# Cross-attention, last batch: softmax denominators of three slots from sums on GpSimd in place of products with ones

## The chip, the cores and the metric

One core of a Trainium2 chip runs the whole kernel. The metric is the device time of one execution in microseconds (us), the median of several runs. The core has TensorE (PE in the profile; PEld are its weight loads), VectorE (DVE), ScalarE (ACT), GpSimd (POOL) and SyncE (SP), which here only starts transfers. Each engine works its own instructions in order and waits for the others by semaphores.

## What is computed

A decoder layer for 8 batches of 224 rows of 512 values, with a context of 750 rows a batch: linear self-attention, cross-attention with 16 heads of 32, and a feed-forward network (FFN) with ternary weights. The change is inside cross-attention:

```python
q = heads(x_q @ w_q)
k, v = heads(x_kv @ w_kv)
logits = q @ k.T * SCALE + (i - j) * w_rel[head]
attn = softmax(logits)            # exp(logits - max) / sum over the 750 keys
x = x + (attn @ v) @ w_proj
```

The "denominator" of a query and head is that sum over keys.

## The kernel before

`cross_attention` works through B = 8 batches b, each in NG = 4 slots s of HG = 4 heads; the text counts slots as n = 4b + s, so the last batch is slots 28 to 31. A slot has 16 beats k. In each beat every engine has a fixed list of work, written out by hand, so that the beats order the engines against each other.

On TensorE a beat holds: one or two halves of the maxima of the *next* slot (`maxima_half`, read by VectorE in `reduce_half`, L1761); in beats 0 to 11 one `logits` (L1952), for key tile pair i = k // 4 and head j = k % 4, into one of two PSUM banks; in beats 5, 9 and 13 an `attend` (L1992) for i = 0, 1, 2; in beat 2 the `denominators` of the slot before (L2002); in beat 12 `turn_maxima`, which waits for VectorE's `join_maxima`; and one part of a projection from a table. In the last batch that table (`last_fill`) holds, besides keys (K) and outputs (Y), the parts W0 to W23: transposes of the FFN's ternary weights. W0 to W3 stand in beats 12 to 15 of slot 28, W4 to W7 in beats 6, 8, 10, 12 of slot 29, W8 to W15 in slot 30, W16 to W23 in beats 0 to 8 of slot 31.

ScalarE turns logits into exponentials (L1652), 125 keys x 448 (two key tiles a = 0, 1 of 224 queries), into one of two buffers of `pT`, i by i in turn. It also copies projections, and in the last batch scales and rounds the FFN weights (`round_weight`, L1643) five beats ahead of their W part, and issues the last six key copies itself at beat 13 of slot 29 (L1683). VectorE makes each rounded weight ternary two beats ahead of its W part (`ternary`, L1783, a TENSOR_SCALAR from SBUF to SBUF), and takes the transposed weight out of PSUM after it (L1725). At beat 2 it divides the slot before: `divide`, a reciprocal (L1774) and a product (L1777). GpSimd splits that result in two parts (`split_heads`, L1526 and L1528).

A denominator is made in one of two ways. In slots 0 to 27 GpSimd adds the six tiles of exponentials of a slot in five additions of 125 x 896 (`sum_keys`, L1543; the text calls them m0 to m4). m0 needs the exponentials of i = 0, m1 and m2 those of i = 1, m3 and m4 those of i = 2. TensorE then multiplies the one sum with ones in `denominators`, four products a slot. ScalarE's exponentials wait for `p_summed`, since the buffers of `pT` come free only when added. In slots 28 to 31 `attend` multiplies every tile with ones too, 24 products a slot, and `divide` waits for `pv_done`:

```python
for col in (0, DEN) if b == B - 1 else (0,):
    for j in range(HG):
        h = HG * s + j
        weights = cv[...] if col == 0 else ones[0:KB, 0:HD]
        last = M.matmul(psO[...], weights, pT[...], ...)
```

In the earlier batches VectorE's `normalise` (L1707), two TENSOR_SCALAR from SBUF to SBUF, comes at beat 12 of slot 3 of a batch, beside `sum_keys`.

The FFN starts behind slot 31. Its first rows are loaded by `first_x` into the space of the sums (`sum_space`), once `den_full` says that the last sum was read; VectorE's `ffn_statistics(0)` reads them at beat 7 of slot 31, and GpSimd's `ffn_prepare(0)` goes on from there.

Of the kernel before, what the change touches and what calls it, by code (L numbers as in the profile page):

```python
# [20 lines left out]
NG = D // P  # L21
# [27 lines left out]
def wait_apart(eng, sem, value, passed):  # L49

    eng.wait_ge(sem, value)
    eng.sem_inc(passed, 1)
# [1138 lines left out]
def cross_attention(nc, sems, sa, x1, ctx_rows, k_rows, q_rows, x2, shared, ffn_weights, w_abs, w_deq, out):  # L1191
# [5 lines left out]
    B, N, _ = x1.shape  # L1197
# [12 lines left out]
    DEN = 256  # L1210
# [2 lines left out]
    LAST_STEP = UNITS - HG  # L1213
    HALVES = 2 * NT * HG
    BEATS = 16
    EXP_BANKS = 2
    PROJ_BANKS = 3


    counts = (2, 1, 1, 1, 1, 1, 1, 2, 2, 1, 2, 1)  # L1220
    halves_at = [range(sum(counts[:k]), sum(counts[:k + 1])) for k in range(BEATS)]
    unit_at = [(k // HG, k % HG) if k < UNITS else None for k in range(BEATS)]
    attend_at = {5: 0, 9: 1, 13: 2}
    DENOMINATORS_AT = 2
# [27 lines left out]
    ]  # L1252
    unit_beat = {int(what[1:]): BEATS * s + k for s in range(NG) for k, what in last_fill[s].items() if what[0] == "W"}
    ROUND_AHEAD, TERNARY_AHEAD = 5, 2
# [24 lines left out]
    def ended_before(b, s, k):  # L1279

        s, k = (s, k - 1) if k > 0 else (s - 1, BEATS - 1)
        b, s = (b, s) if s >= 0 else (b - 1, NG - 1)
        part = part_at(b, s, k) if b >= 0 else None
        return part[:2] if part and part[2] == parts_of[part[0][0]] - 1 else None
# [13 lines left out]
    with ExitStack() as ctx:  # L1298
# [52 lines left out]
        ffn_eps = sb("ffn_eps", [P, 1])  # L1351
        psS = ps("psS", [P, EXP_BANKS, 512])
        psO = ps("psO", [P, 512])
# [14 lines left out]
        p_summed, den_full = sem("p_summed"), sem("den_full")  # L1368
# [8 lines left out]
        def ffn_part(unit):  # L1377

            n, t = weight_of(unit)
            w = ffn_weights[n].rearrange("(a p) k -> p a k", p=P)  # L1380
            src = w[:, 2 * t:2 * t + 2] if n < 2 else w[:, :, 2 * t * P:2 * (t + 1) * P]
            return f_raw[raw_of[unit]].rearrange("p (a k) -> p a k", a=src.shape[1]), src
# [7 lines left out]
        spare, = (n for n in range(PROJ_BANKS) if n not in [bank_of[what, B - 1] for what in ("Y0", "Y1")])  # L1390
        ffn_places = {"ident": ident_b, "magic": magic, "eps_half": ffn_eps, "sums": sum_space, "keys": k_st_space,
                      "packed_k": k4_space, "packed_q": q4_space, "context": c_space, "banks": (psS, psM, psO, psR),
                      "sums_read": den_full, "sums_read_all": NG * (B - 1),
                      "output_banks": [bank_of[what, B - 1] for what in ("Y0", "Y1")],
                      "spare_read": (read[spare], len(order[spare::PROJ_BANKS])),
                      "outputs_read": [(read[bank_of[what, B - 1]], use_of[what, B - 1]) for what in ("Y0", "Y1")],
# [8 lines left out]
        def _(sp):  # L1405
# [38 lines left out]
            def load_ffn(unit):  # L1444

                if unit < 3:
                    sp.wait_ge(pv_done, NB * NG * (B - 1))
                elif unit == 3:
                    for pair in range(2):
                        wait_apart(sp, q_packed[pair], QPACK * B, sp_passed)  # L1450
                elif unit == 4:
                    for what in ("Xa", "Xb"):
                        wait_apart(sp, full[bank_of[what, B - 1]], use_of[what, B - 1], sp_passed)
                elif raw_before[unit] is None:
                    sp.wait_ge(full[bank_of["K3b", B - 1]], use_of["K3b", B - 1])
                else:
                    sp.wait_ge(f_tern_ready, raw_before[unit] + 1)
                dst, src = ffn_part(unit)
                sp.dma_start(dst, src).then_inc(f_in[raw_of[unit]], DMA)
# [36 lines left out]
                    pack_keys(b + 1, 1)  # L1496
                    pack_queries(b + 1, 1)
            ffn_first_x, ffn_rest = ffn_sync(sp)
            ffn_first_x()
            for unit in range(18, UNITS_W):  # L1500
                load_ffn(unit)
            ffn_rest()

        @block.gpsimd
        def _(pool):
# [65 lines left out]
            for b in range(B):  # L1571
                for s in range(NG):
                    if (b, s) != (0, 0):
                        split_heads(*((b, s - 1) if s > 0 else (b - 1, NG - 1)))
                    if s == 1 and b >= 1:
                        store(b - 1)
                    if s == 3 and b + 2 < B:
                        rstd(b + 2)
                    if b + 1 < B:
                        sum_keys(b, s)  # L1580
                    if b + 1 < B:
                        clear_shift(b, s)
                    if s == NG - 1 and b + 2 < B:
                        load_context(b + 2)
# [8 lines left out]
        def _(act):  # L1593
# [51 lines left out]
            def exponentials(b, s, i, j):  # L1645
                n = NG * b + s
                if j == 0 and NB * n + i >= 2:
                    act.wait_ge(pv_done, NB * n + i - 1)
                    if n < NG * (B - 1) or (n == NG * (B - 1) and i < 2):
                        act.wait_ge(p_summed, SUMS * n + (-2, 0, 1)[i])  # L1650
                act.wait_ge(st_full, UNITS * n + HG * i + j + 1)
                nc.scalar.activation(pT[:, (s + i) % 2, j], psS[0:KB, (HG * i + j) % EXP_BANKS, 0:2 * N],  # L1652
                                     ACT.Exp).then_inc(exp_done, 1)
# [9 lines left out]
            for b in range(B):  # L1663
                for s in range(NG):
                    for k in range(BEATS):
                        if ended := ended_before(b, s, k):
# [18 lines left out]
                        if b == B - 1:  # L1685
                            for unit in range(UNITS_W):
                                if unit_beat[unit] - ROUND_AHEAD == BEATS * s + k:
                                    round_weight(unit)
# [3 lines left out]
        def _(dve):  # L1692
# [74 lines left out]
            def divide(b, s):  # L1767

                n = NG * b + s
                if b < B - 1:  # L1770
                    dve.wait_ge(den_full, n + 1)
                else:
                    dve.wait_ge(pv_done, NB * (n + 1))
                V.reciprocal(den[:], psO[:, DEN:DEN + N]).then_inc(den_ready, 1)  # L1774
                dve.wait_ge(den_ready, n + 1)
                wait_count(dve, oT_ready, n)
                V.tensor_tensor(o_f[:], psO[:, 0:N], den[:], ALU.mult).then_inc(o_ready, 1)  # L1777
# [42 lines left out]
            for b in range(B):  # L1820
                for s in range(NG):
                    n = NG * b + s + 1
# [32 lines left out]
        def _(pe):  # L1855
# [86 lines left out]
            def logits(b, s, i, j):  # L1942
# [3 lines left out]
                if i == 0 and j == 0:  # L1946
                    pe.wait_ge(shift_ready, n + 1)
                wait_count(pe, exp_done, unit + 1 - EXP_BANKS)
                for a in range(2):
                    t = 2 * i + a  # L1950
                    col = t * KB if t < NB else t * KB + OVER
                    last = M.matmul(psS[0:KB, (HG * i + j) % EXP_BANKS, a * N:(a + 1) * N], k4[0:ROWS, s % 2, j, col:col + KB],  # L1952
                                    q4[0:ROWS, s, j, :], start=True, stop=True)
# [24 lines left out]
            def attend(b, s, i):  # L1978

                n = NG * b + s  # L1980
                pe.wait_ge(exp_done, UNITS * n + HG * (i + 1))
                if i == 0:
                    pe.wait_ge(w_scale_step, 1) if n == 0 else pe.wait_ge(o_ready, n)
                    for t in range(NK) if s == 0 else ():
                        pe.wait_ge(read[bank_of[f"V{t}", b]], use_of[f"V{t}", b])
                for a in range(2):
                    t = 2 * i + a
                    for col in (0, DEN) if b == B - 1 else (0,):
                        for j in range(HG):
                            h = HG * s + j  # L1990
                            weights = cv[:, b % 2, t, h * HD:(h + 1) * HD] if col == 0 else ones[0:KB, 0:HD]
                            last = M.matmul(psO[HD * j:HD * (j + 1), col:col + N], weights,  # L1992
                                            pT[:, (s + i) % 2, j, a * N:(a + 1) * N], start=t == 0 and col == 0,
                                            stop=t == NK - 1, skip_group_check=True)
                last.then_inc(pv_done, 1)
# [41 lines left out]
            for b in range(B):  # L2037
                for s in range(NG):
                    n = NG * b + s + 1
                    for k in range(BEATS):  # L2040
                        if n < NG * B:
                            for half in halves_at[k]:
                                maxima_half(n, half)
                            if k == TURN_AT:
                                turn_maxima(n)
                        if unit := unit_at[k]:
                            logits(b, s, *unit)
                        if k in attend_at:
                            attend(b, s, attend_at[k])
                        if k == DENOMINATORS_AT and 0 < NG * b + s <= NG * (B - 1):  # L2050
                            denominators(*((b, s - 1) if s > 0 else (b - 1, NG - 1)))
                        if part := part_at(b, s, k):
                            do(*part)
# [61 lines left out]
```

## Time and profile before

| | us |
|---|---|
| median of 3 runs (lowest, highest) | 1256.83 (1255.55, 1259.95) |
| the profiled execution, its own time | 1259.24 |
| its span, first to last instruction | 1257.4 |
| TensorE busy | 1174.2 |
| VectorE busy | 809.4 |
| ScalarE busy | 588.0 |
| GpSimd busy | 541.6 |

The span is what the profile covers; the time of the profiled execution has 1.84 us around it. Busy times overlap. Slot 28 begins at about 979 us of the span, slot 29 at 1002, slot 30 at 1024, slot 31 at 1046, and the FFN at about 1066. Timelines merge neighbouring instructions of one line, and a row's length is then that of the group.

### The profile page before, as it was taken

To read this page: it belongs to the slowest core of one execution; us is meant where nothing else is said; L and a number is where in the kernel's file an instruction comes from. 1 tells how busy PE (TensorE), PEld (TensorE's weight loads), DVE (VectorE), ACT (ScalarE), POOL (GpSimd) and SP (SyncE) were. 2 spreads that over 40 slices of the span, in tenths; PEclk is the share of its full clock that TensorE was granted. 3 is DMA by queue.
4 is the path that set the end of the run, shared out by engine and by line. 5 is a ranking of instruction groups with operands and counts; after the bars stand their busy time and mean duration, and the time that the engine had idled before them with its cause. 6 is when DMAs were issued, how large, how long until landed. Compare 5 with 4: busy or idle time off the path is not lost. (4 is left out here: it accounts for less than half of the span.)

```text
span 1257.4 us, 25102 instructions
## 1 busy us (share of the span) xinstructions
PE 1174.2 (93%) x9456; PEld 903.6 (72%) x9482; DVE 809.4 (64%) x1492; ACT 588.0 (47%) x967; POOL 541.6 (43%) x432
## 2 busy tenths in 40 slices
PE   3799999999799999999999999999999988899997
PEld 3687888887677878778877878878788866344443
DVE  5856666676546666656566665656665677587774
ACT  3222332225235445435444454444454566577775
POOL 0012111115116665656665665765755212354551
PEclk9899999999989999999999999999999989899999
DMA  5311333425524253343343343352532683122121
GB/s 173 96 49 47 102 127 127 143 79 165 134 74 114 51 149 96 73 125 89 80 133 98 82 133 86 97 138 52 134 101 60 202 247 113 42 73 67 58 67 42
DMA packets 76138, 129.43 MB, mean 103 GB/s; under 512 B 18764, under 2 KB 35276, under 8 KB 76027
## 3 DMA queue, kind: packets, MB, share of 16 engines
q1 hardware_dynamic: 63267, 104.28, 30.0%
q0 software_dynamic: 11680, 21.81, 5.4%
q10 hardware_dynamic: 1104, 2.15, 0.6%
q8 instruction: 58, 0.95, 0.3%
q14 instruction: 29, 0.24, 0.1%
HBM read 68.96 MB, written 11.22 MB: 64 GB/s over the span
## 5 line engine op out<-in xcount | busy, mean ns | idle before, releaser
L1761 DVE TENSOR_REDUCE xa_m_part<-xa_psM 112x1 f32<-112x376 f32 x512 | 266.5, 545 | 232.8 <-PE xa_psM L1968 230.3
L1652 ACT ACTIVATE space<-xa_psS 125x448 f32<-125x448 f32 x384 | 208.2, 544 | 180.7 <-PE xa_psS L1952 178.9
L1543 POOL TENSOR_TENSOR xa_sum_space<-xa_sum_space,space 125x896 f32<-125x896 f32 x112 | 238.3, 2128 | 97.3 <-ACT space L1652 92.9
L1968 PE MATMUL xa_psM<-xa_k,xa_q 104*112 104x376 f32 x512 | 162.2, 355 | 16.1 <-DVE xa_m_part L1761 7.6
L1952 PE MATMUL xa_psS<-xa_q,xa_k 104*125 104x224 f32 x768 | 147.3, 274 | 3.4 <-ACT space L1652 3.4
L1952 PEld LDWEIGHTS xa_psS<-xa_q,xa_k 104*125 104x125 f32 x768 | 139.1, 189 | 6.7 <-ACT space L1652 4.5
L1968 PEld LDWEIGHTS xa_psM<-xa_k,xa_q 104*112 104x112 f32 x512 | 87.9, 177 | 36.8 <-DVE xa_m_part L1761 12.9
L1526 POOL TENSOR_SCALAR xa_oT_hi<-xa_o_f 128x224 fp32r<-128x224 f32 x32 | 25.3, 790 | 180.7 <-DVE xa_o_f L1777 180.5
L1992 PE MATMUL xa_psO<-space,cv 125*32 125x224 f32 x1536 | 95.2, 360 | 0.9 <-ACT space L1652 0.9
L1938 PE MATMUL xa_psR<-xa_cT_hi,w_lo 128*128 128x376 f32 x256 | 91.6, 358 | 0.0
L1938 PE MATMUL xa_psR<-xa_cT_hi,w_hi 128*128 128x376 f32 x256 | 86.9, 339 | 1.7 <-DVE xa_cT_lo L1751 1.7
L1938 PE MATMUL xa_psR<-xa_cT_lo,w_hi 128*128 128x376 f32 x256 | 87.4, 341 | 0.0
L61 PE MATMUL sa_psR<-sa_xT_hi,w_hi 128*128 128x224 f32 x256 | 72.7, 284 | 10.8 <-DVE sa_xT_lo L472 10.8
L1938 PE MATMUL xa_psR<-w_hi,xa_cT_hi 128*125 128x512 f32 x192 | 79.9, 416 | 0.0
L1938 PE MATMUL xa_psR<-w_lo,xa_cT_hi 128*125 128x512 f32 x192 | 78.8, 410 | 0.0
L1938 PE MATMUL xa_psR<-w_hi,xa_cT_lo 128*125 128x512 f32 x192 | 76.6, 399 | 0.0
L1543 POOL TENSOR_TENSOR xa_sum_space<-space 125x896 f32<-125x896 f32 x28 | 59.7, 2132 | 28.6 <-ACT space L1652 24.2
L61 PE MATMUL sa_psR<-sa_xT_lo,w_hi 128*128 128x224 f32 x256 | 71.3, 279 | 0.0
L61 PE MATMUL sa_psR<-sa_xT_hi,w_lo 128*128 128x224 f32 x256 | 71.1, 278 | 0.0
L1595 ACT ACTIVATE cv<-xa_psR 125x512 f32<-125x512 f32 x48 | 28.7, 598 | 88.5 <-PE xa_psR L1938 88.5
L1992 PEld LDWEIGHTS xa_psO<-space,cv 125*32 125x32 f32 x1536 | 40.2, 109 | 30.7 <-issue 11.0
L1938 PEld LDWEIGHTS xa_psR<-xa_cT_hi,w_lo 128*128 128x128 f32 x256 | 49.1, 192 | 18.3 <-issue 18.3
(214 smaller groups left out, 2662.0 us busy)
## 6 DMA issues: line engine op xcount, KB each, us to landing
xa_k<-xa_k_st SPq DMA_DIRECT2D x378, 94.0 KB, 2.2
xa_q<-xa_q_st SPq DMA_DIRECT2D x192, 56.0 KB, 2.0
cv<-in_ctx_dram POOLq DMA_DIRECT2D x7, 1500.0 KB, 21.5
cv<-in_L_ffn_w_gate_dram SPq DMA_DIRECT2D x14, 512.0 KB, 4.7
cv<-in_L_ffn_w_down_dram SPq DMA_DIRECT2D x10, 512.0 KB, 7.0
cv<-in_L_ffn_w_up_dram SPq DMA_DIRECT2D x9, 512.0 KB, 6.0
sa_x_raw<-in_x_dram SPq DMA_DIRECT2D x8, 448.0 KB, 6.1
sa_rows<-in_x_dram SPq DMA_DIRECT2D x8, 448.0 KB, 4.0
```

The lines of the kernel that those rows point to most:

```text
L61: ins = nc.tensor.matmul(out, left(i, c), right(j, c), start=first and n == 0, stop=last and n == len(terms) - 1)
L1526: nc.gpsimd.tensor_scalar(oT_hi[:, s], o_f[:], 1.0, None, ALU.mult).then_inc(oT_hi_ready, 1)
L1543: nc.gpsimd.tensor_tensor(p_sum[:], before, tile, ALU.add).then_inc(p_summed, 1)
L1595: return nc.scalar.activation(out, in_, ACT.Copy, scale=scale)
L1652: nc.scalar.activation(pT[:, (s + i) % 2, j], psS[0:KB, (HG * i + j) % EXP_BANKS, 0:2 * N], ACT.Exp).then_inc(exp_done, 1)
L1761: V.tensor_reduce(m_part[:, t, jj, seg:seg + 1], psM[0:T, seg, 0:SEG], AX.X, ALU.max).then_inc(mx_read, 1)
L1938: last = M.matmul(out, left(i, k), right(j, k), start=m == 0, stop=m == len(terms) - 1)
L1952: last = M.matmul(psS[0:KB, (HG * i + j) % EXP_BANKS, a * N:(a + 1) * N], k4[0:ROWS, s % 2, j, col:col + KB], q4[0:ROWS, s, j, :], start=T ...
L1968: M.matmul(psM[0:T, seg, 0:SEG], q4[0:ROWS, g, jj, t * T:(t + 1) * T], k4[0:ROWS, g % 2, jj, seg * SEG:(seg + 1) * SEG], start=True, stop= ...
L1992: last = M.matmul(psO[HD * j:HD * (j + 1), col:col + N], weights, pT[:, (s + i) % 2, j, a * N:(a + 1) * N], start=t == 0 and col == 0, sto ...
```

## The change

Slots 28, 29 and 30 get their denominators as all slots before do: five additions on GpSimd, and four products of their sum with ones at beat 2 of the next slot. `attend` makes products with ones in slot 31 alone. ScalarE's exponentials of these slots wait for `p_summed`, `divide` of slots 28 to 30 waits for `den_full`, and the first load of FFN rows waits for `den_full` 31 in place of 28; on SyncE it is moved behind the loads of the weight parts 18 to 23.

```diff
--- before.py
+++ after.py
@@ -1213,6 +1213,7 @@
     LAST_STEP = UNITS - HG
     HALVES = 2 * NT * HG
     BEATS = 16
+    LAST = NG * B - 1
     EXP_BANKS = 2
     PROJ_BANKS = 3
 
@@ -1390,7 +1391,7 @@
         spare, = (n for n in range(PROJ_BANKS) if n not in [bank_of[what, B - 1] for what in ("Y0", "Y1")])
         ffn_places = {"ident": ident_b, "magic": magic, "eps_half": ffn_eps, "sums": sum_space, "keys": k_st_space,
                       "packed_k": k4_space, "packed_q": q4_space, "context": c_space, "banks": (psS, psM, psO, psR),
-                      "sums_read": den_full, "sums_read_all": NG * (B - 1),
+                      "sums_read": den_full, "sums_read_all": LAST,
                       "output_banks": [bank_of[what, B - 1] for what in ("Y0", "Y1")],
                       "spare_read": (read[spare], len(order[spare::PROJ_BANKS])),
                       "outputs_read": [(read[bank_of[what, B - 1]], use_of[what, B - 1]) for what in ("Y0", "Y1")],
@@ -1496,9 +1497,9 @@
                     pack_keys(b + 1, 1)
                     pack_queries(b + 1, 1)
             ffn_first_x, ffn_rest = ffn_sync(sp)
-            ffn_first_x()
             for unit in range(18, UNITS_W):
                 load_ffn(unit)
+            ffn_first_x()
             ffn_rest()
 
         @block.gpsimd
@@ -1576,7 +1577,7 @@
                         store(b - 1)
                     if s == 3 and b + 2 < B:
                         rstd(b + 2)
-                    if b + 1 < B:
+                    if NG * b + s < LAST:
                         sum_keys(b, s)
                     if b + 1 < B:
                         clear_shift(b, s)
@@ -1646,7 +1647,7 @@
                 n = NG * b + s
                 if j == 0 and NB * n + i >= 2:
                     act.wait_ge(pv_done, NB * n + i - 1)
-                    if n < NG * (B - 1) or (n == NG * (B - 1) and i < 2):
+                    if n < LAST or i < 2:
                         act.wait_ge(p_summed, SUMS * n + (-2, 0, 1)[i])
                 act.wait_ge(st_full, UNITS * n + HG * i + j + 1)
                 nc.scalar.activation(pT[:, (s + i) % 2, j], psS[0:KB, (HG * i + j) % EXP_BANKS, 0:2 * N],
@@ -1767,7 +1768,7 @@
             def divide(b, s):
 
                 n = NG * b + s
-                if b < B - 1:
+                if n < LAST:
                     dve.wait_ge(den_full, n + 1)
                 else:
                     dve.wait_ge(pv_done, NB * (n + 1))
@@ -1985,7 +1986,7 @@
                         pe.wait_ge(read[bank_of[f"V{t}", b]], use_of[f"V{t}", b])
                 for a in range(2):
                     t = 2 * i + a
-                    for col in (0, DEN) if b == B - 1 else (0,):
+                    for col in (0, DEN) if n == LAST else (0,):
                         for j in range(HG):
                             h = HG * s + j
                             weights = cv[:, b % 2, t, h * HD:(h + 1) * HD] if col == 0 else ones[0:KB, 0:HD]
@@ -2047,7 +2048,7 @@
                             logits(b, s, *unit)
                         if k in attend_at:
                             attend(b, s, attend_at[k])
-                        if k == DENOMINATORS_AT and 0 < NG * b + s <= NG * (B - 1):
+                        if k == DENOMINATORS_AT and NG * b + s > 0:
                             denominators(*((b, s - 1) if s > 0 else (b - 1, NG - 1)))
                         if part := part_at(b, s, k):
                             do(*part)
```

## Rows read from the trace of the kernel before

**Rows 1.** The page, costliest groups: xcount | busy us, mean ns | idle before, releaser.
```profile
L1761 DVE TENSOR_REDUCE xa_m_part<-xa_psM 112x1 f32<-112x376 f32 x512 | 266.5, 545 | 232.8 <-PE xa_psM L1968 230.3
```

**Rows 2.** Windows of slots 28, 29, 30: length, PE, PEld, DVE, ACT, POOL busy us, clock.
```profile
979.10:1002.30 23.20, 23.20 (x228) 18.80 (x226) 15.97 (x30) 12.99 (x20) 2.49 (x4) 1.00 0.63 192
...
1002.30:1023.70 21.40, 18.24 (x199) 14.62 (x195) 16.62 (x32) 12.26 (x19) 2.95 (x3) 1.00 0.76 225
...
1023.70:1046.20 22.50, 19.41 (x204) 14.99 (x204) 19.33 (x36) 18.42 (x24) 1.67 (x2) 0.85 1.07 316
```

**Rows 3.** Timeline of TensorE: start, us, line, what, [idle before <- releaser].
```profile
981.94 0.58 PE L2002 MATMUL xa_psO<-xa_sum_space,ones 125*32 125x224 f32 x8
...
986.30 0.56 PE L1992 MATMUL xa_psO<-space,ones 125*32 125x224 f32 x8
...
986.68 0.56 PE L1992 MATMUL xa_psO<-space,cv 125*32 125x224 f32 x8
...
1002.28 0.57 PE L1968 MATMUL xa_psM<-xa_k,xa_q 104*112 104x376 f32 x2
...
1023.66 0.60 PE L1968 MATMUL xa_psM<-xa_k,xa_q 104*112 104x376 f32 x2 [1.12 <-DMA xa_k<-xa_k_st]
...
1027.27 0.76 PE L1952 MATMUL xa_psS<-xa_q,xa_k 104*125 104x224 f32 x2 [1.56 <-ACT space L1652]
```

**Rows 4.** Timeline of ScalarE, last batch.
```profile
993.56 0.54 ACT L1652 ACTIVATE space<-xa_psS 125x448 f32<-125x448 f32 x1
...
998.11 0.53 ACT L1652 ACTIVATE space<-xa_psS 125x448 f32<-125x448 f32 x1
...
1013.24 0.54 ACT L1652 ACTIVATE space<-xa_psS 125x448 f32<-125x448 f32 x1 [1.09 <-PE xa_psS L1952]
...
1020.56 3.81 ACTq L1683 DMA_DIRECT2D xa_k<-xa_k_st  x6
...
1042.08 0.54 ACT L1652 ACTIVATE space<-xa_psS 125x448 f32<-125x448 f32 x1 [0.35 <-PE xa_psS L1952]
```

**Rows 5.** Timeline of VectorE, last batch.
```profile
997.08 0.69 DVE L1783 TENSOR_SCALAR xa_x_space<-cv 128x1024 bf16<-128x1024 f32 x1
...
1000.14 0.68 DVE L1725 TENSOR_SCALAR w_all<-xa_psR 128x1024 bf16<-128x1024 bf16 x1
...
1000.74 0.68 DVE L1783 TENSOR_SCALAR xa_x_space<-xa_q_st_space 128x1024 bf16<-128x1024 f32 x1
...
1008.78 0.68 DVE L1783 TENSOR_SCALAR xa_x_space<-xa_xn 128x1024 bf16<-128x1024 f32 x1
...
1012.31 0.69 DVE L1783 TENSOR_SCALAR xa_x_space<-cv 128x1024 bf16<-128x1024 f32 x1
...
1015.33 0.68 DVE L1783 TENSOR_SCALAR xa_x_space<-cv 128x1024 bf16<-128x1024 f32 x1
...
1034.89 0.55 DVE L1761 TENSOR_REDUCE xa_m_part<-xa_psM 112x1 f32<-112x376 f32 x1 [1.33 <-PE xa_psM L1968]
...
1043.59 0.68 DVE L1783 TENSOR_SCALAR xa_x_space<-cv 128x1024 bf16<-128x1024 f32 x1
...
1056.69 0.69 DVE L1725 TENSOR_SCALAR w_all<-xa_psR 128x1024 bf16<-128x1024 bf16 x1 [0.62 <-PE xa_psR L1895]
```

**Rows 6.** Timeline of GpSimd: additions of slot 3 and of slot 27.
```profile
444.12 4.51 POOL L1543 TENSOR_TENSOR xa_sum_space<-xa_sum_space,space 125x896 f32<-125x896 f32 x2 [2.38 <-ACT space L1652]
...
975.01 4.31 POOL L1543 TENSOR_TENSOR xa_sum_space<-xa_sum_space,space 125x896 f32<-125x896 f32 x2 [2.38 <-ACT space L1652]
```

**Rows 7.** Line 1707: duration in ns, shortest, median, longest.
```profile
L1707 DVE TENSOR_SCALAR xa_xn<-xa_xn,xa_x_mv,xa_x_rs x16: 531/545/2344, 313.4 to 886.8; 112x512 f32<-112x512 f32 x16
```

**Rows 8.** Timeline of VectorE in slot 3.
```profile
443.85 2.80 DVE L1707 TENSOR_SCALAR xa_xn<-xa_xn,xa_x_mv,xa_x_rs 112x512 f32<-112x512 f32 x2
```

**Rows 9.** Timeline of GpSimd in slot 29.
```profile
1008.55 1.44 POOL L1528 TENSOR_TENSOR xa_oT_lo<-xa_o_f,xa_oT_hi 128x224 fp32r<-128x224 f32 x1
```

**Rows 10.** Window of TensorE: length, busy us, granted clock, DMA share, GB/s.
```profile
1028.00:1030.00 2.00, 2.00 (x14) 0.50 1.04 280
```

## Prediction

> **What bounds the kernel now.** I read the page first. TensorE is its busiest engine, and the costliest group of instructions is VectorE's reduce of the maxima, L1761, which TensorE feeds and waits for by turns [rows 1]. But the change touches only the last batch of cross-attention, slots 28 to 31 (slot n = 4b + s), so what bounds those counts. The windows by slot give it [rows 2]: slot 28 has TensorE busy for 23.20 of 23.20 us and GpSimd for 2.49; slot 29 has TensorE at 18.24 of 21.40, VectorE at 16.62; slot 30 has TensorE at 19.41 of 22.50, VectorE at 19.33, ScalarE at 18.42. So slot 28 is bound by TensorE, and slot 30 by three engines in lock-step. GpSimd is nearly idle in all three. The timelines of single engines then show who hands to whom: in slots 29 and 30 TensorE stands still before the first logits of slot 30 for a packed key and then for ScalarE, which comes from issuing the key copies [rows 3, 4]; and VectorE works without a break from the end of slot 30 on, with the idle time 0.62 us near its last transposed weight of slot 31 [rows 5].
>
> **What is removed and added on TensorE.** A group of four products with ones takes 0.38 us of TensorE (the next group starts 986.68 - 986.30 later) [rows 3]. Six groups a slot are 2.28 us, three slots 6.84 us. Slots 29, 30 and 31 each get one `denominators` at beat 2: 0.58 us by the one of slot 27, which stands there already for batch 6 [rows 3], say 0.6 with its entry, together 1.8 us. If TensorE alone counted, the change would be worth -5.0 us.
>
> **What is added on GpSimd.** Five additions a slot at 4.31 / 2 = 2.15 us [rows 6], 10.8 us a slot, in slots 28 to 30. GpSimd has the time (2.49 and 2.95 of its 23.20 and 21.40 us are used [rows 2]), and no consumer waits for it directly: additions m3 and m4 start when the last exponential of the third pair ends and need 4.5 us, while beat 2 of the next slot comes over 6 us after it (998.64 against slot 29's start at 1002.28 plus two beats) [rows 3, 4]. The new wait of `exponentials` at beat 8 needs only the first addition, which is through two to four beats earlier. The load of the first FFN rows moves behind `den_full` 31, beat 2 of slot 31; five beats remain before `ffn_statistics(0)` reads them, on queues then empty. These I cost at nothing; if GpSimd ran 3 us late they would begin to count.
>
> **What is not free: VectorE.** In batches 0 to 5 `normalise` issues two TENSOR_SCALAR of 112x512, SBUF to SBUF. Of the 16 on record the shortest took 531 ns and the longest 2344 [rows 7]. The pair at 443.85 took 2.80 us together [rows 8]; the second of it fell on an addition that GpSimd had begun at 444.12 [rows 6]. It ended only after that addition's 2.15 us, and the two additions stretched from 4.31 to 4.51. The same 2.80 (once 2.79) stands in all six batches that have it, of which one is shown. So a VectorE tensor_scalar from SBUF waits for a running addition to end, gets in before the next one, and pushes that one by about 0.2 to 0.35 us. PSUM readers don't: L1761 keeps a mean of 545 ns over all its 512, with additions running beside most of them [rows 1]. The last batch is where VectorE has just such instructions: 24 `ternary`, 128x1024 SBUF to SBUF, 0.68 us [rows 5], in beats 10 to 13 of slot 28, 4, 6, 8, 10 of slot 29, ten of slot 30, six of slot 31. TensorE's W parts wait for each two beats later, in order with everything else it does.
>
> I walk them through, in the times of before.
> Slot 28: TensorE leads by 0.76 us after beat 5 and 1.52 after beat 9. The exponential that frees m1 ends at 993.56 + 0.54 - 0.76 = 993.3, so m1 runs 993.5 to 995.7, m2, m3 and m4 follow without a gap to about 1003.3 (the data of m3 is there at 998.64 - 1.52 = 997.1). The first ternary comes at 997.08 - 1.52 = 995.6 and passes at once. The second comes, behind a reduce and `join_maxima`, at 997.0 and gets in when m2 ends, 998.4; the third at the end of m3, 1000.8; the fourth, behind one take of 0.6 us, at the end of m4, 1003.2, and ends at 1003.9. W3 needs it, so TensorE enters slot 29 at about 1004.4 in place of 1002.28 [rows 3, 5]: **+2.1**, where it should have been -2.3.
> Slot 29: the ternary of 1012.31 (beat 6) falls at the start of m0 (which follows the split of the heads and the store by 0.3 us): held about 1.8. That of 1015.33 falls in m1, which begins 0.2 after the exponential's end at 1013.78 and ends at 1016.1 [rows 4, 5]: held 0.7. The other two fall between the pairs. TensorE saves 2 x 0.76 and pays 0.6 up to beat 12: -0.9. Together **+1.6**, and the third 0.76 goes into the wait for the packed key. By then ScalarE's issue of the key copies at 1020.56, the start of slot 30's chain, is 3.7 late [rows 4].
> Slot 30: `divide` waits for `denominators`, which stands behind the logits of 1027.27 (0.76, then 0.6 to 0.9 at that clock): 1.3 late, and the idle 1.33 us of VectorE before 1034.89 takes that up [rows 3, 5]. One ternary of beats 4 and 5 is held by m0, 1.0 or 2.0 according to which of the two comes first: 1.5. m1 and m2 end just when ternaries come: 0.1. The ternary of 1043.59 falls in m3 (from 0.2 after 1042.62 to 1045.0) [rows 4, 5], 1.4, and the next in m4, 1.2, of which 0.7 goes into a gap. VectorE is busy from there to 1056.07, where 0.62 more is taken up: 1.3. TensorE's saving in this slot is hidden, since it isn't the later one. **+2.9**.
> Slot 31 keeps its products with ones; the FFN starts behind `ffn_statistics(0)`, which is behind those takes on VectorE. Sum: 2.1 + 1.6 + 2.9 = 6.6; I take **+7**, because close races that I gave to the ternary can only add. The profiled execution (1259.24 us, span 1257.4) would be 1266.2; the median of the runs, 1256.83, becomes 1263.8.
> The holds are bounded below by nothing (a ternary that hits no addition) and above by one whole addition, 2.15 us less the work that stands between: at most some 14 of the 24 meet one.
>
> A row disagrees a little with a strict lock: at 1008.55 GpSimd's subtraction took 1.44 us, about twice its usual time, and the ternary that began 0.23 later kept its 0.68 [rows 5, 9]. The later of the two went first. The Trainium skill ("SBUF — State Buffer", Who interferes with whom) has it that whichever of the two engines starts first holds the shared ports for the whole instruction and the other fully blocks. By that rule every close race is lost to the addition and the sum would be about 8; by the row some are won and it would be about 6.
>
> **Rivals.**
> A, forecast: the holds add up over the three slots, +4 to +10. For it: six held pairs of six, and ternaries two beats ahead of TensorE.
> B, only slot 28 pays: its +2.1 stands, but in slots 29 and 30 TensorE's savings (1.7 each at most) count and the holds go into the idle time that VectorE has there (4.8 and 3.2 us) [rows 2]. -1.3 to +3.8; 1256 to 1260.6. Against it: the idle time lies in pieces, mostly elsewhere than at the holds.
> C, forecast and a clock loss: the grant stood at 0.50, the 1.2 GHz level, from 1028 on [rows 10], after TensorE had been idle for pieces of 1.1 to 1.6 us [rows 3]. The holds of slot 28 put pieces of 0.5, 1.9 and 1.9 us right ahead of slot 29, whose first six beats are TensorE's own work. Three to six microseconds at half rate cost 1.5 to 3: +8.5 to +12, 1265 to 1269. The Trainium skill ("TensorE: Matmul & The Clock Gate", Part 1) describes a gate that puts an idle array to 1.2 GHz until it has been busy again; the rows agree, and don't say where it would strike.
> D, faster: ternaries don't collide, as additions and ternaries fall into each other's gaps. Then TensorE's -5.0 counts, less what slot 30 hides: -2.3 to -5.0, 1252 to 1254.5. It decides for D if the second to fourth ternary of slot 28 are held less than 0.8 us each. Against it: four additions in a row cover all four.
>
> **How the numbers follow.** A 0.56, B 0.20, C 0.14, D 0.10. A measurement of this kernel tells 0.3%, 3.8 us, from no change. Slower: nearly all of A and C, 0.69; same: B and the lowest of A, 0.21; faster: D, 0.10. The time is A's, 1263.8. The range leaves out D and the upper end of C: 1255.5 to 1270; A's own is 1260.8 to 1266.8.
>
> **What the profile of after would show.** Right: L1783 with a mean well over 0.68 us and a longest near 2.5; products with ones on L1992 in slot 31 alone; 15 more additions on L1543, at 2.1 to 2.5 us; slot 29 starting over 1 us later than 1002.28; TensorE waiting for L1783 in slot 28, where it waited for nothing. Wrong: L1783 still at 0.68; slot 29 starting before 1001; or a wait of TensorE for `xa_sum_space` at beat 2, which would put the loss on GpSimd's pace and not on the held ternaries.

## The result, and the profile after

The change makes the kernel slower: 1262.75 us in the median of 20 runs against 1255.99 of 20 runs of the kernel before on the same chip, a ratio of 1.0047 with a 95% interval of 1.0034 to 1.0059, about +5.9 us (+4.3 to +7.4). The forecast was +7, with a range for the time of 1255.5 to 1270.

The page of the profiled execution (1263.9 us, span 1262.2), the busy times and the group that answers to [rows 1]:

```profile
PE 1173.5 (93%) x9362; PEld 901.1 (71%) x9362; DVE 816.6 (65%) x1492; ACT 589.0 (47%) x967; POOL 574.9 (46%) x447
...
L1762 DVE TENSOR_REDUCE xa_m_part<-xa_psM 112x1 f32<-112x376 f32 x512 | 266.6, 545 | 228.5 <-PE xa_psM L1969 225.6
```

GpSimd has 15 instructions and 33.3 us more than before. VectorE has the same 1492 instructions and yet 7.2 us more. The reduce of the maxima keeps its 545 ns, so the 7.2 us are elsewhere. The timeline of VectorE after, the rows that answer to [rows 5]; L1784 is `ternary`, L1726 the take of a transposed weight:

```profile
994.00 0.69 DVE L1784 TENSOR_SCALAR xa_x_space<-cv 128x1024 bf16<-128x1024 f32 x1
...
996.46 1.99 DVE L1784 TENSOR_SCALAR xa_x_space<-cv 128x1024 bf16<-128x1024 f32 x1
998.37 0.68 DVE L1726 TENSOR_SCALAR w_all<-xa_psR 128x1024 bf16<-128x1024 bf16 x1
998.97 1.96 DVE L1784 TENSOR_SCALAR xa_x_space<-xa_q_st_space 128x1024 bf16<-128x1024 f32 x1
...
1012.87 1.91 DVE L1784 TENSOR_SCALAR xa_x_space<-cv 128x1024 bf16<-128x1024 f32 x1
...
1037.43 1.57 DVE L1784 TENSOR_SCALAR xa_x_space<-xa_c_space 128x1024 bf16<-128x1024 f32 x1
...
1047.65 1.89 DVE L1784 TENSOR_SCALAR xa_x_space<-cv 128x1024 bf16<-128x1024 f32 x1
...
1050.06 1.97 DVE L1784 TENSOR_SCALAR xa_x_space<-cv 128x1024 bf16<-128x1024 f32 x1
```

And the timeline of GpSimd after, additions of the last batch:

```profile
984.94 2.12 POOL L1544 TENSOR_TENSOR xa_sum_space<-space 125x896 f32<-125x896 f32 x1 [0.20 <-POOL xa_oT_lo L1529]
988.82 4.34 POOL L1544 TENSOR_TENSOR xa_sum_space<-xa_sum_space,space 125x896 f32<-125x896 f32 x2 [1.76 <-ACT space L1653]
995.74 4.64 POOL L1544 TENSOR_TENSOR xa_sum_space<-xa_sum_space,space 125x896 f32<-125x896 f32 x2 [2.58 <-ACT space L1653]
...
1012.12 2.10 POOL L1544 TENSOR_TENSOR xa_sum_space<-space 125x896 f32<-125x896 f32 x1
1015.07 4.68 POOL L1544 TENSOR_TENSOR xa_sum_space<-xa_sum_space,space 125x896 f32<-125x896 f32 x2 [0.85 <-ACT space L1653]
...
1035.92 2.53 POOL L1544 TENSOR_TENSOR xa_sum_space<-space 125x896 f32<-125x896 f32 x1 [0.20 <-POOL xa_oT_lo L1529]
```

Six of the 24 ternaries take 1.57 to 1.99 us in place of 0.68, together 7.2 us more, which is all that VectorE gained. Such a ternary is called held from here on, and what it takes over its 0.68 us is its hold. Each begins inside an addition and ends about half a microsecond after it: the one of 996.46 lies in the first of the pair that began at 995.74. The take at 998.37, which reads PSUM, lies inside the second of that pair and keeps 0.68 us. An addition behind a held ternary is late: the pair takes 4.64 in place of 4.34 us.

Who waits for it is in the waits of TensorE over the last batch after:

```profile
PE xa_psR L1896 <- DVE xa_x_space L1784: 6.5, 7, 1.9
PE xa_psS L1953 <- ACT space L1653: 3.9, 1, 3.9
PE xa_psM L1969 <- DVE xa_m_part L1762: 2.7, 3, 2.1
```

Before, the first of these was 0.5 us, once. The three longest stops of TensorE in the last batch after, from its timeline:

```profile
1001.08 0.61 PE L1896 MATMUL xa_psR<-xa_ident_b,xa_x_space 128*128 128x128 bf16 x8 [1.88 <-DVE xa_x_space L1784]
...
1015.29 0.95 PE L1969 MATMUL xa_psM<-xa_k,xa_q 104*112 104x376 f32 x2 [2.10 <-DVE xa_m_part L1762]
...
1030.03 0.76 PE L1953 MATMUL xa_psS<-xa_q,xa_k 104*125 104x224 f32 x2 [3.89 <-ACT space L1653]
```

The first is for the held ternary of 998.97, the second for a reduce that stood behind the held one of 1012.87. The third is for ScalarE, which comes from issuing the key copies; before, TensorE stopped for it for 1.56 us, and for 1.12 just ahead for a packed key [rows 3].

The waits bring a second loss. Windows of TensorE over the last batch (length, busy us, granted clock, DMA share, GB/s), the kernel before:

```profile
1027.20:1034.10 6.90, 6.83 (x55) 0.53 1.07 332
1034.10:1050.60 16.50, 13.25 (x178) 1.00 0.86 243
1050.60:1054.00 3.40, 3.40 (x25) 0.51 0.02 5
```

and after:

```profile
1002.40:1005.80 3.40, 3.40 (x14) 0.51 0.40 155
...
1016.20:1019.60 3.40, 3.40 (x30) 0.53 1.00 342
...
1029.90:1040.10 10.20, 9.74 (x64) 0.51 1.07 308
1040.10:1053.80 13.70, 9.59 (x110) 0.99 0.58 187
1053.80:1057.20 3.40, 3.40 (x30) 0.54 0.13 19
```

Before, TensorE was granted 1.2 GHz for 10.3 us of its last batch; after, for 20.4 us, in four stretches. Two of them, at 1002.4 and 1016.2, are new, and each comes right behind one of the first two stops above.

To place the loss, `turn_maxima` (beat 12 of each slot) and the first transpose of the FFN serve as marks, since the two executions enter the last batch at different times. TensorE's timeline, before:

```profile
975.01 0.36 PE L1975 MATMUL xa_psM<-ident,xa_m_neg 112*4 112x112 f32 x2
...
998.57 0.36 PE L1975 MATMUL xa_psM<-ident,xa_m_neg 112*4 112x112 f32 x2
...
1020.09 0.35 PE L1975 MATMUL xa_psM<-ident,xa_m_neg 112*4 112x112 f32 x2 [1.08 <-DVE xa_m_neg L1765]
...
1043.13 0.35 PE L1975 MATMUL xa_psM<-ident,xa_m_neg 112*4 112x112 f32 x2 [1.08 <-DVE xa_m_neg L1765]
...
1066.17 0.38 PE L1129 MATMUL xa_psR<-xa_ident_b,xa_k_st_space 128*128 128x128 bf16 x4 [0.67 <-POOL xa_k_st_space L936]
```

and after:

```profile
973.46 0.36 PE L1976 MATMUL xa_psM<-ident,xa_m_neg 112*4 112x112 f32 x2
...
995.49 0.36 PE L1976 MATMUL xa_psM<-ident,xa_m_neg 112*4 112x112 f32 x2
...
1001.50 0.58 PE L1969 MATMUL xa_psM<-xa_k,xa_q 104*112 104x376 f32 x2
...
1022.46 0.35 PE L1976 MATMUL xa_psM<-ident,xa_m_neg 112*4 112x112 f32 x2 [1.08 <-DVE xa_m_neg L1766]
...
1047.19 0.35 PE L1976 MATMUL xa_psM<-ident,xa_m_neg 112*4 112x112 f32 x2 [1.08 <-DVE xa_m_neg L1766]
...
1071.47 0.38 PE L1129 MATMUL xa_psR<-xa_ident_b,xa_k_st_space 128*128 128x128 bf16 x4 [0.73 <-POOL xa_k_st_space L936]
```

| from mark to mark, us | before | after | |
|---|---|---|---|
| slot 27 beat 12 to slot 28 beat 12 | 23.56 | 22.03 | -1.5, TensorE's saving |
| to slot 29 beat 12 | 21.52 | 26.97 | +5.5 |
| to slot 30 beat 12 | 23.04 | 24.73 | +1.7 |
| to the first FFN transpose | 23.04 | 24.28 | +1.2 |
| together | 91.16 | 98.01 | +6.9 |

The last batch holds the whole loss. (The spans differ by 4.8 only: the execution before entered this batch 1.55 us later, and the rest is in the FFN.)

### The profile page after: what moved, and what is told of

Read it like the earlier page. It is cut to its first block and busy times, and to the rows that moved or that the text cites. A ratio compares the mean times of both kernels' runs of the same rounds, so it can differ in the third digit from the quotient of the medians.

```text
span 1262.2 us, 24914 instructions
## 1 busy us (share of the span) xinstructions
PE 1173.5 (93%) x9362; PEld 901.1 (71%) x9362; DVE 816.6 (65%) x1492; ACT 589.0 (47%) x967; POOL 574.9 (46%) x447
## 5 line engine op out<-in xcount | busy, mean ns | idle before, releaser
L1544 POOL TENSOR_TENSOR xa_sum_space<-xa_sum_space,space 125x896 f32<-125x896 f32 x124 | 264.8, 2135 | 108.7 <-ACT space L1653 103.8
L1544 POOL TENSOR_TENSOR xa_sum_space<-space 125x896 f32<-125x896 f32 x31 | 66.5, 2144 | 28.9 <-ACT space L1653 24.0
```

Of the source, the lines that this page charges most:

```text
L1544: nc.gpsimd.tensor_tensor(p_sum[:], before, tile, ALU.add).then_inc(p_summed, 1)
```

## The experiments

Each kernel below was run 12 times, beside runs of the kernel before. A ratio stands with its 95% interval, and a difference in us is the ratio less 1, times 1257. An interval of 0.002 to either side is 2.5 us. The edits are shown by the lines that decide; "..." marks what is left out, mostly counts of the waits that follow from these lines. "Leg" is a stretch from mark to mark as in the table above.

**Slot 28 alone.** The change with additions in slot 28 only:

```diff
+    FROM_SUMS = lambda n: n < NG * (B - 1) or n in (28,)
...
-                    if NG * b + s < LAST:
+                    if FROM_SUMS(NG * b + s):
                         sum_keys(b, s)
...
-                    for col in (0, DEN) if n == LAST else (0,):
+                    for col in (0,) if FROM_SUMS(n) else (0, DEN):
```

> Only slot 28 takes its denominators from additions; slots 29 and 30 keep products with ones. Theory (held ternaries): the third and fourth ternary of slot 28 are held about 1.3 us each, slot 29 starts 0.5 to 1 us later than before, and the half clock at its start adds 1 to 2 us: +1 to +3 us, of the +6.8 of the whole change. Rival (clock alone, through the removed products): the same sign only if TensorE falls to half clock without a held ternary. Rival (GpSimd's pace and the later divide): -1.6 us.

Measured: 1.0013 (0.9996 to 1.0029), +1.6 us (-0.5 to +3.6). Two ternaries of slot 28 take 1.98 and 1.96 us, no other is held. The size is the theory's, and the -1.6 of GpSimd's pace lies outside the interval. That this slot alone makes the kernel slower isn't shown by the times, since the interval holds 0; in its profile the leg over the two holds took 25.91 us in place of 21.52.

**Slot 29 alone.** The same with `n in (29,)`.

> Only slot 29 from additions. Theory: one ternary (beat 6) is held about 1.2 us by the first addition, against a saving of 0.9: 0 to +2 us, the upper end if TensorE's longer wait brings the half clock. Rival (GpSimd's pace, the later divide in slot 30): +1.3 us in slot 30, where denominators stands behind logits that waited for ScalarE.

Measured: 1.0036 (1.0016 to 1.0056), +4.5 us (+2.0 to +7.0), more than either had. One ternary takes 2.13 us in place of 0.68, held by the first addition. This slot alone costs most of what the change costs, and a single hold of 1.45 us can't be all of it; see slot 29 with small additions below. GpSimd's and VectorE's timelines of this run also have a race that came out the other way:

```profile
1008.37 5.23 POOL L1546 TENSOR_TENSOR xa_sum_space<-xa_sum_space,space 125x896 f32<-125x896 f32 x2 [0.32 <-ACT space L1657]
...
1010.96 0.68 DVE L1788 TENSOR_SCALAR xa_x_space<-cv 128x1024 bf16<-128x1024 f32 x1
```

The second of this pair of additions began at 1010.65, 0.31 us ahead of the ternary, and took 2.95 us, while the ternary kept its 0.68.

**Slot 30 alone.** The same with `n in (30,)`.

> Only slot 30 from additions. Theory: three ternaries held, 0.9 + 1.2 + 1.3 us, none of it covered: +2 to +4 us. Rival (clock alone): 0, since TensorE was at half rate in slot 30 before. Rival (later divide in slot 31): at most +1.

Measured: 0.9998 (0.9983 to 1.0013), -0.3 us (-2.1 to +1.6). Three ternaries are held (1.56, 1.87, 1.99 us), as foreseen, and yet no cost shows. So the holds of slot 30 are covered or paid back, which falls against my walk. The three slots alone sum to +5.8, with some 3.7 us of uncertainty either way, and the change is +5.9.

**Small additions.** The change, with its additions of the last batch cut to 2 columns of 224 a head. Instructions, waits, denominators and TensorE's work stay; the result isn't the sum.

```diff
+                    width = N if b < B - 1 else 2
-                    nc.gpsimd.tensor_tensor(p_sum[:], before, tile, ALU.add).then_inc(p_summed, 1)
+                    nc.gpsimd.tensor_tensor(p_sum[:, :, 0:width], before[:, :, 0:width], tile[:, :, 0:width], ALU.add).then_inc(p_summed, 1)
```

> The change, but the additions of slots 28 to 30 cover 2 of 224 columns a head, so their result is not the sum; order, waits, denominators and removed products are all as in the change. Theory: without long additions no ternary is held (longest under 0.9 us), and TensorE's saving shows: -2.3 to -5 us against before, 9 to 12 us faster than the change. Rival (clock, through the removed products) and rival (later divide, beat-2 denominators): both are still in it, so it stays slower than before by 3 us or more.

Measured: 0.9995 (0.9978 to 1.0012), -0.6 us. No ternary is over 0.81 us. The loss is gone, so it comes from the length of the additions: neither the clock through missing products nor the waits explain +5.9. The first load of FFN rows has moved in this run as in the change, so it doesn't either. But the saving of 2.3 to 5 us doesn't show either. By the marks it is there at first: 22.03 and 20.27 us to beat 12 of slot 29, 2.8 less than before; then 24.42 and 24.95 give 3.3 back. VectorE now has a wait (in all, times, longest) that it hardly had before, nearly all of it in slots 30 and 31:

```profile
DVE xa_den L1776 <- PE xa_psO L2004: 3.9, 3, 1.9
```

The division of slot 29 in VectorE's timeline of this run:

```profile
1022.41 1.00 DVE L1763 TENSOR_REDUCE xa_m_part<-xa_psM 112x1 f32<-112x376 f32 x2
1025.12 1.56 DVE L1776 RECIPROCAL xa_den<-xa_psO 128x224 f32<-128x224 f32 x1 [1.70 <-PE xa_psO L2004]
```

Before, `divide` of slots 29 and 30 ran on VectorE while TensorE's logits of beat 2 waited for ScalarE. Now it needs `denominators`, and those stand behind just these logits. Whether that is what gives the saving back is put to a run below.

**Half additions.** The same with 112 columns of 224.

> The change, but the additions of slots 28 to 30 cover 112 of 224 columns a head (their result is not the whole sum), so each lasts about 1.1 us. Theory: a hold is at most what is left of an addition, so it shrinks from about 1.3 to under 0.6 us, and fewer ternaries meet one: the time lies between the change and the one with small additions, -3 to +2 us against before. Rival (number of instructions or of waits on GpSimd): as the change, +6.

Measured: 0.9999 (0.9977 to 1.0022), -0.1 us (-2.9 to +2.8). The longest ternary is 1.03 us, a hold of 0.35. With half the columns no loss is left that the times show, though number, order and waits of the additions are those of the change. Half the way from -0.6 to +5.9 would be +2.7, at the edge of the interval, so that the price grows faster than the length is likely, not shown.

**Additions besides.** The change's additions and ScalarE's waits for them, but TensorE keeps the products with ones and the denominators come from those.

```diff
-                    for col in (0, DEN) if n == LAST else (0,):
+                    for col in (0, DEN) if b == B - 1 else (0,):
...
-                        if k == DENOMINATORS_AT and NG * b + s > 0:
+                        if k == DENOMINATORS_AT and 0 < NG * b + s <= NG * (B - 1):
```

> Additions of slots 28 to 30 run on GpSimd with the same waits of ScalarE, but TensorE keeps all products with ones and the denominators come from them, so the sums are not used. Theory: the holds are there without the saving: +7 to +12 us. Rival (clock through removed products) and rival (later divide): nothing of theirs is in it, 0.

Measured: 1.0063 (1.0039 to 1.0088), +7.9 us (+4.9 to +11.1), inside the theory's range and far from the rivals' 0. Additions alone do the harm. From VectorE's timeline of this run, the two ternaries of slot 28:

```profile
996.81 2.00 DVE L1785 TENSOR_SCALAR xa_x_space<-cv 128x1024 bf16<-128x1024 f32 x1
...
999.33 1.96 DVE L1785 TENSOR_SCALAR xa_x_space<-xa_q_st_space 128x1024 bf16<-128x1024 f32 x1
```

**The load moved.** The kernel before with the first load of FFN rows behind the weight loads, as in the diff.

> The kernel before, with the first load of FFN rows behind the loads of weight parts 18 to 23. All theories that leave the load out: 0 (within 0.15%). Were the load the cause, +2 us or more, with VectorE waiting for the rows before its first FFN statistics.

Measured: 1.0000 (0.9974 to 1.0026), 0.0 us (-3.3 to +3.3). The interval leaves room for 3 us. But in this run's profile VectorE doesn't wait ahead of its first FFN statistics, and the small additions above, which have the load moved too, show no loss. So the load is not what costs the +5.9.

**Clear additions.** Of slot 28 tiles 0 to 3 are added, of slot 29 tiles 2 to 5; the other tiles, and slot 30, keep products with ones.

```diff
+    added = lambda n: range(NK) if n < NG * (B - 1) else range(0, 4) if n == LAST - 3 else range(2, 6) if n == LAST - 2 else ()
...
-                for m in range(SUMS):
-                    i, a = divmod(m + 1, 2)
+                for m, t in enumerate(added(n)[1:]):
+                    i, a = divmod(t, 2)
```

> Only those tiles are added on GpSimd whose additions met no ternary in the profile of the change: in slot 28 tiles 0 to 3 (three additions), in slot 29 tiles 2 to 5 (three); the other tiles of these slots, and slots 30 and 31, keep their products with ones. Theory: no ternary is held over 0.3 us, TensorE saves 2 x 1.52 us less 2 x 0.6: -1 to -2 us. Rival (clock or later divide): 0 to +2.

Measured: 1.0011 (0.9988 to 1.0034), +1.4 us, which tells nothing apart: the theory's -1 to -2 and the rivals' 0 to +2 both touch the interval (-1.5 to +4.3). A ternary of slot 29 is still held (1.28 us), since without its first addition the slot's beats moved; a profile's gaps don't stand still.

**Small additions, denominators at beat 1.**

```diff
-                        if k == DENOMINATORS_AT and NG * b + s > 0:
+                        if k == (DENOMINATORS_AT if NG * b + s <= NG * (B - 1) else 1) and NG * b + s > 0:
```

> As the run with small additions (2 of 224 columns a head, so not the sum), with TensorE's denominators of slots 28 to 30 at beat 1 in place of beat 2, ahead of the logits that wait for ScalarE. Theory (late divide): there VectorE waited 1.70 and 1.95 us for the denominators before it could divide in slots 30 and 31, where before it divided while TensorE waited; with beat 1 these waits go, and TensorE's saving shows: -2.5 to -4 us against before. Rival (slots 30 and 31 are bound by ScalarE's issue of key copies and roundings and by the transfers, so that no saving on TensorE can show): as with beat 2, -1 to 0.

Measured: 0.9974 (0.9956 to 0.9993), -3.3 us (-5.5 to -0.9), and VectorE's wait for the denominators is down to 0.2 us. The row that answers to the one of 1025.12 above has no wait:

```profile
1022.55 1.00 DVE L1763 TENSOR_REDUCE xa_m_part<-xa_psM 112x1 f32<-112x376 f32 x2
1023.47 1.55 DVE L1776 RECIPROCAL xa_den<-xa_psO 128x224 f32<-128x224 f32 x1
```

TensorE's saving is real once nothing holds the ternaries and the division isn't late. How much the late division cost isn't shown: this run and the one with beat 2 differ by 2.6 us, with some 3 us of uncertainty either way. By the marks the leg to beat 12 of slot 30 fell from 24.42 to 21.64 us when the wait went. The leg behind it did not: it takes 24.95 us with the wait and 24.73 without, against 23.04 before. So what is given back there is not the division's. What these two have in common is that TensorE was granted 1.2 GHz for 6.8 us of this leg, against 3.4 before. The six profiles of this record with 6.8 us there took 24.73 to 25.09 us for the leg, and slot 29 alone with small additions, which has none there, took 22.76. Each is a single execution, and none says why the low stretch was longer.

**The change, denominators at beat 1.** The same edit on the whole change.

> The change with denominators of slots 28 to 30 at beat 1. Theory (held ternaries and, besides, the late divide): the holds stay, about six of 1.3 us, and the wait for the denominators goes: +3 to +5 us against before, 2 to 3.5 less than the change. Rival (the late divide costs nothing): +6 to +7, as the change.

Measured: 1.0037 (1.0018 to 1.0057), +4.7 us (+2.3 to +7.2). The six holds are there (ternaries of 1.55 to 2.16 us) and VectorE's wait for the denominators is gone. It is 1.2 us better than the change, less than foreseen and within the uncertainty; in the change this wait was 1.7 us in slot 30 and short in slot 31. And here TensorE stopped 0.57 us at beat 1 of slot 30 for the sum itself, the one place in these runs where GpSimd's pace shows.

**Tiles 0 to 3 of slot 28 alone, denominators at beat 1.** As "clear additions", with `added` empty for slot 29.

> Only tiles 0 to 3 of slot 28 are added on GpSimd (three additions that end before its first ternary), their denominators at beat 1 of slot 29; all else as before. Theory: no hold, TensorE saves 1.52 less 0.6: -1.5 to 0 us, hardly to be told from no change. Rival (any addition in the last batch costs): +1 or more.

Measured: 0.9992 (0.9974 to 1.0009), -1.0 us (-3.3 to +1.1). No hold, and no loss. So an addition in the last batch isn't harmful as such. As a version it isn't shown to be faster.

**Slot 29 alone, small additions.** The run with slot 29 alone, with additions of 2 columns (not the sum).

> Slot 29 alone, as in the run with slot 29 from additions, but the additions cover 2 of 224 columns a head (not the sum). What differs is the length of the additions only. Theory (held ternary, with the half clock that the wait behind it brings): from +4.5 us down to 0 to +1.5 (saving 1.5, later divide +1.5 in slot 30). Rival (the later divide and the extra denominators are the price of slot 29): +3 to +5, as with full additions.

Measured: 0.9992 (0.9971 to 1.0014), -1.0 us (-3.6 to +1.8), against +4.5 with whole additions: 5.5 us apart, with some 3.7 us of uncertainty either way. Nothing differs but the length of five additions. Window over the last batch, slot 29 with whole additions:

```profile
974.00:1066.00 92.00, 80.51 (x776) 0.87 0.60 185
```

The same window, slot 29 with small additions:

```profile
974.00:1066.00 92.00, 80.13 (x799) 0.94 0.60 186
```

The granted clock over these 92 us is 0.87 with the hold and 0.94 without. VectorE's wait for the denominators is 1.7 us at its longest in both, so the late division is not the price of slot 29; and in neither does the profile show TensorE or ScalarE waiting for an addition in this batch, so GpSimd's pace isn't either.

One execution can't show that a hold brings the low clock, but the profiles of all 14 kernels agree on it. Take the leg from beat 12 of slot 28 to beat 12 of slot 29. In five kernels a hold of over 1.2 us falls in it: the change, the change with beat 1, slot 28 alone, slot 29 alone, additions besides. All five were granted 1.2 GHz for 3.4 or 6.8 us of it and took 23.45 to 27.29 us. The other nine had 2.4 GHz throughout and took 20.01 to 22.24. No run has such a hold and keeps the clock, so how the loss divides between the two isn't shown.

## Why the prediction was right, point by point

The mechanism was right: additions hold ternaries, and the loss goes when the additions are short. The size, +7 against +5.9, is in part luck: slots 28 and 30 were taken too dear and slot 29 too cheap, and the errors cancel. By slots alone: +2.1 foreseen and +1.6 measured, +1.6 and +4.5, +2.9 and -0.3.

- **TensorE's -5.0.** Right as work: the leg over slot 28's first two `attend` shows the saving (-1.5, foreseen 2 x 0.76) to a hundredth. What remains of it when nothing is held and the division is early is -3.3 us (small additions, beat 1).
- **The hold itself.** Right, and read from `normalise` [rows 7, 8]: 2344 ns there, up to 1.99 us for a ternary here, and 2.16 in one run. Shown by the small additions: same instructions and waits, no hold, no loss. That L1761 was not held while additions ran "beside most of them" is misread, since in the trace of before 176 of its 512 have one beside them; but these 176 have a mean of 546 ns too, so the conclusion stands.
- **Slot 28, +2.1.** Mis-sized: +0.8 (1001.50 - 977.55 against 1002.28 - 979.10). The failed step is "the exponential that frees m1 ends at 993.56 + 0.54 - 0.76". That row [rows 4] is the exponential of beat 9; m1 needs the one of beat 7, about 3 us earlier. So m1 and m2 ran from 988.82 to 993.2, ahead of the first ternary at 994.00, and two ternaries were held in place of three. The same error stands behind "four additions in a row cover all four", against rival D.
- **Slot 29, +1.6.** Mis-sized: from its start to its beat 12 it took 20.96 in place of 17.81 us, +3.2. The hold at beat 6 came, with 1.2 us in place of 1.8; the one in m1 didn't. In its place came what stood under rival C with 0.14: TensorE stopped 1.88 us for a weight before slot 29 and 2.10 us at beat 7, and worked 6.8 us of this slot at 0.51 and 0.53 of its clock. By the runs with slot 29 alone, one hold costs 5.5 us (+4.5 against -1.0, each with its interval) and goes with a granted clock over the batch of 0.87 in place of 0.94. A and C were one case, and I should have given the clock much more weight. C's own sum also has a slip: 7 and 1.5 to 3 make +8.5 to +10, and nothing stands behind its +12. The Trainium skill ("TensorE: Matmul & The Clock Gate", Part 1) says that an idle array drops to 1.2 GHz and needs work to return. The rows agree in this: the grant fell behind stops of 0.85 and 1.88 us and of 2.10 us, and rose again behind stretches in which TensorE was busy throughout.
- **Slot 30, +2.9.** The three holds came (0.89, 1.21 and 1.29 us, foreseen 1.5, 1.4 and 1.2), but the slot alone measures -0.3 us, where three holds sum to 3.4. In the change it took +1.7 to its beat 12 and +1.2 from there. What failed is the share of the holds that goes into gaps, put at 0.7 and 0.62 us; which waits take up the rest isn't shown. In the one profile of slot 30 alone the leg to its beat 12 took 22.37 us and the leg behind it 24.37, against 23.04 and 23.04 before, with the low clock for 3.4 us of each in place of 6.8 and 3.4. So part may have been paid back by the clock; a single execution can't say more.
- **`divide` 1.3 late, "taken up".** The wait was 1.70 us in slot 30, and nothing shows that it was taken up where no ternary is held: the small additions without it are at -3.3 us, with it at -0.6. The two intervals overlap, and part of the difference lies in a leg where the clock differed too.
- **GpSimd's waits and the load at nothing.** Right as far as measured: no wait of TensorE for `xa_sum_space` after, and 1.0000 for the load, known to 3.3 us.
- **The race rows [rows 9].** After, the same pattern stands again: at 1009.62 the subtraction took 1.44 us beside a ternary of 0.68. The Trainium skill ("SBUF — State Buffer", Who interferes with whom) says that whoever issues first gets the shared ports for the whole instruction and the other fully blocks. By these rows an operation of GpSimd whose record begins 0.24 us earlier still loses, and so does the addition of slot 29 alone that began 0.31 us earlier. But of `normalise` in the earlier batches the second instruction of the pair at 443.85 begins at 444.31, 0.19 us behind the start of an addition [rows 6, 8], and was the one that waited. So the recorded starts alone don't tell who wins, and what does isn't shown; for a close race a sum needs both outcomes. That the other blocks fully agrees with the rows here: 1.99 against 0.68 us for `ternary`. The take, which reads PSUM, kept 0.68 inside an addition.

## What to carry to other kernels

Before work is moved to an idle GpSimd, list what VectorE runs beside it: here a tensor_scalar from SBUF to SBUF waited for the rest of the addition that it met, in all but close races, and the longest instance of such a line in the old trace (2344 ns against a median of 545) showed the price in advance. Shorter additions took it away here; they did less work too, and whole additions split in two weren't run. When TensorE stops for another engine, look at its clock behind the stop too. And where a result is made by a later step, as in `denominators`, look at what stands ahead of that step in its engine's order.

## What the runs showed that was not expected

- The price of a hold hangs on the place: 5.5 us (uncertain by 3.7) for one in slot 29, and -0.3 us (uncertain by 1.9) in all for a slot with three, in slot 30.
- By length of the additions the differences are -0.6 us at 2 columns, -0.1 at 112, +5.9 at 224.
- An operation of GpSimd whose record begins 0.24 or 0.31 us ahead of a ternary can still be the one that waits.
